# Cross-attention and feed-forward kernel: context rows transposed by DMA instead of by TensorE

## What is computed

```
x = x + mlstm_cell(layernorm(x), ctx, ctx)       # gated, causal, 4 heads of 64
x = x + layernorm(x) @ ternary(W).T              # 256 x 256
x = x + softmax(q @ k.T / 16) @ v                # q = layernorm(x) @ Wq; k, v = ctx @ Wkv
x = x + bitlinear(silu(gate) * up, w_down)       # 1024 inner features, 8-bit rows, ternary weights
```

## Time and profile before

| | us |
|---|---|
| median of 3 runs | 677.48 |
| the profiled execution | 679.77 |
| its span, first to last instruction | 677.9 |
| TensorE busy | 636.8 (94%) |
| VectorE busy | 568.9 (84%) |
| ScalarE busy | 524.9 (77%) |
| GpSimd busy | 394.2 (58%) |

### The profile page before, as it was taken

One profiled execution on the slowest core, in us unless ns is written; L12 is line 12 of the kernel. 1 busy time (PEld: TensorE's weight loads), 2 busy tenths in 40 slices (PEclk: granted clock), 3 DMA queues, 4 the chain that ended last, 5 costly groups with the idle time before them and its releaser, 6 DMA issues.

```text
span 677.9 us, 14933 instructions
## 1 busy us (share of the span) xinstructions
PE 636.8 (94%) x4689; PEld 475.0 (70%) x4710; DVE 568.9 (84%) x1481; ACT 524.9 (77%) x1302; POOL 394.2 (58%) x636
## 2 busy tenths in 40 slices
PE   5889999999999999999999999989799999999995
PEld 4668788787887878878778787777355555555563
DVE  4787978888898898887988889887899998899892
ACT  4666787887877869688687777766589988988984
POOL 3355464464644746547455474472467787777775
PEclk9999999999999999999999999999899999999997
DMA  8310202122022120221212201024336868766763
GB/s 297 108 57 7 94 1 94 57 70 95 16 95 72 54 95 20 92 83 44 94 40 87 94 17 64 19 60 156 71 71 163 171 156 170 136 164 160 167 133 110
DMA packets 105409, 63.64 MB, mean 94 GB/s; under 512 B 52845, under 2 KB 105070, under 8 KB 105334
## 3 DMA queue, kind: packets, MB, share of 16 engines
q1 hardware_dynamic: 98470, 59.29, 32.5%
q10 hardware_dynamic: 6864, 3.41, 1.7%
HBM read 29.39 MB, written 20.97 MB: 74 GB/s over the span
## 4 chain that ended last, share of the span: by engine, by line
PE 60%; DVE 14%; ACT 13%; DMA 5%; issue 4%; SPq 2%; POOL 1%; POOLq 0%; DVEq 0%; ACTq 0%
PE bank L704 10%; PE bank L621 9%; PE bank L672 8%; PE bank L651 8%; PE bank L723 5%; DMA us<-usq 4%; PE bank L693 4%; ACT ew L865 4%; PE bank L526 3%; PE bank L589 3%; ACT x2T L832 2%; PE bank L580 2%; DVE st L1239 2%; PE bank L665 2%; PE bank L571 2%
## 5 line engine op out<-in xcount | busy, mean ns | idle before, releaser
L704 PE MATMUL bank<-WGU,fqT 128*128 128x512 bf16 x491 | 122.0, 383 | 7.3 <-DVE vg L1544 3.7
L1110 POOL TENSOR_SCALAR_AFFINE_SELECT D<-D 128x512 f32<-128x512 f32 x64 | 38.4, 636 | 127.4 <-ACT D L856 127.4
L1544 DVE SCALAR_TENSOR_TENSOR vg<-bank,fback,D 128x1024 f32<-128x1024 f32 x64 | 82.0, 1281 | 11.8 <-ACT D L1016 5.7
L704 PEld LDWEIGHTS bank<-WGU,fqT 128*128 128x128 bf16 x512 | 46.9, 98 | 61.5 <-DVE vg L1544 24.0
L1016 ACT ACTIVATE D<-bank,fback 128x1024 f32<-128x1024 f32 x64 | 71.7, 1120 | 19.6 <-PE bank L704 19.6
L1551 DVE TENSOR_REDUCE hmax<-vg 128x1 f32<-128x1025 f32 x64 | 78.1, 1221 | 2.2
L1095 POOL TENSOR_TENSOR rs<-ve,minus_half 128x4 f32<-128x4 f32 x64 | 65.3, 1027 | 22.8 <-DVE ve L1245 20.4
L1196 POOL TENSOR_SCALAR wtmp<-vg,hscale 128x1024 f32<-128x1024 f32 x64 | 71.6, 1119 | 5.8
L1239 DVE BATCH_NORM_STATS2 st<-x 128x6 f32<-128x256 f32 x184 | 64.4, 411 | 2.7
L672 PE MATMUL bank<-W0T,x1T 128*128 128x256 f32 x256 | 60.1, 388 | 2.6 <-DVE C L1346 2.6
L651 PEld LDWEIGHTS bank<-vaug,C 128*128 128x128 f32 x512 | 60.7, 192 | 2.1 <-issue 1.3
(11 more groups left out here) (198 smaller groups left out, 1524.1 us busy)
## 6 DMA issues: line engine op xcount, KB each, us to landing
out_dram<-x SPq DMA_DIRECT2D x30, 512.0 KB, 3.3
xg<-in_x_dram SPq DMA_DIRECT2D x16, 512.0 KB, 3.9
cg<-in_ctx_dram SPq DMA_DIRECT2D x16, 512.0 KB, 4.5
xg<-out_dram SPq DMA_DIRECT2D x8, 512.0 KB, 4.7
cg<-out_dram SPq DMA_DIRECT2D x8, 512.0 KB, 5.5
rows_q<-fq ACTq DMA_DIRECT2D x13, 256.0 KB, 2.3
raw<-in_L_ffn_w_gate_dram SPq DMA_DIRECT2D x1, 1024.0 KB, 8.2
nrm<-in_L_ffn_w_up_dram SPq DMA_DIRECT2D x1, 1024.0 KB, 10.2
```

What stands on the lines that cost most here:

```text
L704: mm = pe.matmul(ps[k + half], fqT[:, i // 2 % 2, c, i % 2 * P:(i % 2 + 1) * P], WGU[:, c, which, half * 512:(half + 1) * 512], start=(c = ...
L1544: dve.scalar_tensor_tensor(out=fh[i % 2][:, 0:INNER], in0=up, scalar=fback[:, g % 2, s, 1:2], in1=fsil[:, i % 2, :], op0=ALU.mult, op1=ALU ...
```

## The change

- From turn n = 2 on, TensorE no longer transposes ctx (TC leaves the body of the loop; it stays in turns 0 and 1), and ScalarE no longer copies it.
- ScalarE, at the end of turn n, splits ctx of group n + 1 into its low and high 16-bit halves (split_ctx, two copies of 128x1024 into ctx_halves).
- SyncE issues two transposing DMAs (ctx_transposes) of 128x1024 16-bit elements, from ctx_halves into halves_turned (the memory of fhT). They stand between load and load_x of the same group.
- GpSimd joins the halves in qcT (join_ctx, two copies), behind power(0) and shifts(0) of turn n. TensorE's VG waits for it.
- T1 becomes the first stage of a turn, with its copies first on ScalarE. A turn has 46 bank uses instead of 48, so the banks rotate, and the banks after the loop are renumbered.

```diff
-STAGES = ("TB", "TC", "DX", "MB", "QK", "T1", "F0", ...
-NEW = {"TC", "TX", "VG", "GA", "TA"}
+STAGES = ("T1", "TB", "TC", "DX", "MB", "QK", "F0", ...
+NEW = {"TX", "VG", "GA", "TA"}
...
+        ctx_halves = sb("ctx_halves", [P, 2, GB * E], U16)
...
+        halves_turned = flat(fhT).bitcast(U16).rearrange("p (w k t) -> p w k t", w=2, t=P)
...
+            def ctx_transposes(g):
+                hold("sp", sp, ctx_split, 2 * g - 2)
+                for w in range(2):
+                    sp.dma_start_transpose(halves_turned[:, w, :, :],
+                                           ctx_halves[:, w, :]).then_inc(ctx_turned, 16)
...
                     load(z + 3, 1 - p)
+                    ctx_transposes(z + 3)
                     load_x(z + 3, 1 - p)
                     store(z)
...
                         for b in range(GB):
                             o = open_("VG", b)
-                            moved("TC", b // 2)
+                            if "TC" in bank.stages:
+                                moved("TC", b // 2)
+                            elif b == 0:
+                                pe.wait_ge(ctx_joined, 2 * n - 2)
...
+            def split_ctx(g):
+                pg = g % 2
+                act.wait_ge(c_in[pg], 8 * (g - pg) + 16)
+                if g > 2:
+                    act.wait_ge(ctx_turned, 32 * (g - 2))
+                for w in range(2):
+                    src = flat(cg).bitcast(U16).rearrange("p (q i w) -> p q i w", q=2, w=2)[:, pg, :, w]
+                    act.activation(ctx_halves[:, w, :], src, ACT.Copy).then_inc(ctx_split, 1)
...
+                if z is not None:
+                    turned_copies(bank, "T1", x1T)
                 if m is not None:
                     key_copy(bank, "TB", keyT[q][:, 1, :])
...
-                if n is not None:
+                if "TC" in bank.stages:
                     half_copies("TC", EC)
...
-                if z is not None:
-                    turned_copies(bank, "T1", x1T)
...
                 if y is not None:
                     scale_rows(y, (2, 3))
 
+                if n is not None and 1 <= n < NG - 1:
+                    split_ctx(n + 1)
...
+            def join_ctx(g):
+                pool.wait_ge(ctx_turned, 32 * (g - 1))
+                for w in range(2):
+                    dst = qcT[g % 2][:, EC:2 * EC, :, :].bitcast(U16).rearrange("p c b (t w) -> p b c t w", w=2)[:, :, :, :, w]
+                    pool.tensor_copy(dst, halves_turned[:, w, :, :].rearrange("p (b c) t -> p b c t", c=EC)).then_inc(ctx_joined, 1)
...
                     power(0, n)
                     shifts(0, n)
+                if z is not None and n is not None:
+                    join_ctx(n)
```

More of the change, by code:

```diff
@@ L35 @@
 BF16 = mybir.dt.bfloat16
-STAGES = ("TB", "TC", "DX", "MB", "QK", "T1", "F0", "UA", "TX", "UB", "VG", "T2", "SC", "TA", "GA", "WT", "O",
+U16 = mybir.dt.uint16
+STAGES = ("T1", "TB", "TC", "DX", "MB", "QK", "F0", "UA", "TX", "UB", "VG", "T2", "SC", "TA", "GA", "WT", "O",
           "WG", "WU", "WD")
-NEW = {"TC", "TX", "VG", "GA", "TA"}
+NEW = {"TX", "VG", "GA", "TA"}
 MID = {"TB", "DX", "MB", "QK", "UA", "UB"}
@@ L115, in last_places @@
     count = [sum(1 for i in range(start) if i % BANKS == k) for k in range(BANKS)]
-    one, two = (4, 5, 6, 7), (0, 1, 2, 3)
-    a = Places({"TB": (6,), "DX": (7, 0, 1, 2), "MB": (3,), "QK": (4, 5, 6, 7), "T1": two, "UA": (4, 5), "UB": (6, 7),
+    one, two = (0, 1, 2, 3), (4, 5, 6, 7)
+    a = Places({"TB": (2,), "DX": (3, 4, 5, 6), "MB": (7,), "QK": (0, 1, 2, 3), "T1": two, "UA": (0, 1), "UB": (2, 3),
                 "F0": two, "T2": one, "SC": one, "WT": one, "O": one}, count)
@@ L120, in last_places @@
     return a, b
-assert (len(FIRST) + len(SECOND) + sum(len(body(z)) for z in range(NG - 2))) % BANKS == 6
+assert (len(FIRST) + len(SECOND) + sum(len(body(z)) for z in range(NG - 2))) % BANKS == 2
 def build(nc, x, ctx_in, ig_w, ig_b, fg_w, fg_b, out_w, w0, wq, wkv, w_gate, w_up, w_down, out):
@@ L281, in build @@
         vaug_ready = sem("vaug_ready")
+        ctx_split = sem("ctx_split")
+        ctx_turned = sem("ctx_turned")
+        ctx_joined = sem("ctx_joined")
         gstep = sem("gstep")
@@ L356, in hold @@
             eng.sem_inc(held[name], 1)
-        bG, bU, bank_o = 4, 6, [ps[2], ps[3]]
+        bG, bU, bank_o = 0, 2, [ps[6], ps[7]]
         gate, up = (banks[:, k:k + 2, :].rearrange("p k n -> p (k n)") for k in (bG, bU))
-        bank_h = [ps[k].bitcast(F16) for k in (0, 1)]
+        bank_h = [ps[k].bitcast(F16) for k in (4, 5)]
         x2_last, x3_last = hh, qn
@@ L411, in _ @@
             load(2, 0)
+            ctx_transposes(2)
             load_x(2, 0)
@@ L419, in _ @@
             load(NG - 1, 1)
+            ctx_transposes(NG - 1)
             load_x(NG - 1, 1)
```

## The result

The changed kernel takes 775.23 us (median of 4 runs, 772.52 to 776.66) beside 677.76 us for the kernel before on the same chip: ratio 1.1425, 95% interval 1.1398 to 1.1452. It is 14% slower, +97.5 us. The profiled execution has a span of 773.2 us against 677.9. The forecast was 755, with a range of 715 to 792.

The account below looks back on a forecast made before the run. A turn was taken as a TensorE-bound front plus a back of about 12 us chained through three engines. Late x 5.0 and clock 0.3 us, by 14 turns, plus 3 us gave +77: 755 us, range 715 to 792.

Parts of the forecast that it names:

- Queue order, the step that decides: SyncE: load of x waits behind split and two transposing issues, issuing at 222.7 instead of 214.45, landing at 226.8.
- The links of the loop: ScalarE's end, split, SyncE, x, VectorE, GpSimd, qn, VG, ScalarE's end: a closed loop, 32.6 us long.
- the sum: All turns: 5.0 us late x plus 0.3 clock, by 14 turns 74 us, plus 3 for weight copies: +77.
- Two terms of that link: SyncE and DMA: each transposing issue 2.1 us (bounds 1.19, 2.38); x landing 4.1 us after its issue (3.9, 5.3).
- The clock: TensorE at half clock behind its gap before UA, most of it hidden: 0.3 us a turn, bounds 0 and 1.5.
- Rival 3: TensorE stays at half clock through UA, TX, UB and much of VG: 2 us a turn, 783 us; chance 0.08.
- The low end of the sum: Issues of 1.19, landing 3.9, no clock cost: 3.0 us a turn, 42 us, 720 us.
- the high end: Issues of 2.38, landing 5.3, split 2.5, clock 1.5, join 0.5: 9.3 us a turn, 130 us, 810 us.
- TC's gain: TensorE: eight transposes fewer per turn from n = 2, 0.87 us; 12.2 us in fourteen turns if nothing else is late.
- T1's move: T1's eight transposes go from behind QK to the turn's head, their ScalarE copies first; ScalarE's change put at nothing.
- rival 2: The halves are late, not x: VG waits for transposes or GpSimd's join; 32 us more, 787 to 790; chance 0.10.
- Rival 1: The load of x isn't late enough to matter, TC's transposes are simply won: 665 us; chance 0.04.

Follow-up runs that it names:

- 1: The changed kernel with SyncE issuing load_x ahead of the two transposing DMAs of the same group: 675.92 us, ratio 0.9977 to the kernel before.
- 6: The changed kernel with unused 128x512 matmuls added ahead of F0 in every turn: 789.71 us with ten, 736.55 us with four.
- 4: The changed kernel, load of x still late, with T1 and its copies back behind QK and the decays: 793.38 us, ratio 1.1712.
- 9: The kernel of 1 with GpSimd's power(0), shifts(0) ahead of power(1), and ScalarE's split ahead of weight copies and last two scale_rows: 668.32 us.
- 5: The kernel before with load_x behind the store in SyncE's queue, without split, transposes or join: 738.34 us, ratio 1.089.

## Why the prediction was right, and where it wasn't

**Queue order, the step that decides: right, and shown.** The exchange in 1 removes the whole loss, and nothing else differs between the two kernels. The links of the loop, the first two from the turn at 293, the others from the short turn before it: end of scale_rows to x landed 291.10 to 300.65, 9.55 us (10.4 in the sum); x to qn 3.85 (3.8); qn to VG 6.4 in the short turn (5.7); VG to ScalarE's end 12.0 there (12.7). They add up to 31.8, and turns with little or no time at the low clock take 31.0 to 31.7, where the sum had 32.6. TensorE's gap in front of UA is 3.6 us in the mean (46.7 by 13), not 4.5 to 5.

**Two terms of that link were mis-sized.** A transposing issue takes 1.32 us and not 2.1: the price is nearly one per instruction, the lower of the two bounds. It was the row of 1.19 us at half the size and not the doubling of it that held. The 1.9 us that the prediction estimated from the Trainium skill, page "DMA: Bandwidth & Descriptors", section "Why a DMA increments its semaphore by 16 and not by 1", was too high as well: the issues here took 1.32. Two issues make -1.6 us a turn. The other way, the load lands in a median of 4.7 us instead of the 4.1 taken, inside its bounds:

```profile
L418 SPq DMA_TRANSPOSE fhT<-ctx_halves x28: 1232/1320/1413, 48.0 to 505.1; - x28
```

```profile
L413 SPq DMA_DIRECT2D xg<-in_x_dram x14: 521/526/1497, 50.7 to 506.5; - x14
...
DMA to landing us min/median/max: 4.2/4.7/5.4
```

**The clock: the term that was furthest off.** The sum had 0.3 us a turn, bounds 0 and 1.5; the runs show 2.7 in the mean (38 by 14), above the dear bound. I had read three microseconds at half clock behind a gap of 2.37 from the one place in which the kernel before shows it, carried the length over, and called most of it hidden, because ScalarE comes to UA's products late. Here the low level lasts 3.4 us in one turn and 13.7 in another, after gaps of nearly the same length. What works at half speed in the long ones is exactly the chain from UA to VG, on which ScalarE waits: qn to VG takes 9.0 us there (6.4) and VG to ScalarE's end 14.2 (12.0). Rival 3 had the mechanism and nearly the price, 2 us a turn more than the sum where it is 2.4, with a chance of 0.08. Why one turn gets the clock back after 3.4 us and the next after 13.7 stays open.

The Trainium skill, page "TensorE: Matmul & The Clock Gate", section "HAM oscillation — how this bites in real kernels", says that the half rate comes back in every pass of a loop in which TensorE idles between bursts. The trace agrees: the granted clock is 0.77 to 0.95 in each of the 13 turns. What it would cost here had to be measured.

**Whole sum.** At full clock the change costs 736.55 - 676.91 = 59.6 us (6, which still has the late x), where the sum without its clock term had 73; the clock costs 38, where it had 4. The errors, -13 and +34, cancel in part, and the time came out 20 us above the forecast and inside a range that was made wide for the unknown prices. That is partly luck: 775.2 lies just above the narrower range, 720 to 775, to which I had given most of the chance, and without the first error it would have come near 789. (The low end of the sum, 720, also leaves out the 3 us of the turns with weight copies that the high end has.)

**TC's gain and T1's move.** TC's 0.87 us a turn is TensorE time, and with the queue mended 0.65 of it arrives (27.60 to 26.95). "At nothing" for T1's move was wrong: alone it costs 6.8 us, by the way from its copies over decays, GpSimd's powers and qn to the gate rows. I had followed ScalarE's own idle time and not who waits for the decays. In the change itself the move helps (4), since F0 then runs inside the wait for x.

**ScalarE and GpSimd.** The split takes 1.90 us (2.0 in the sum). In the turns without weight copies it is covered, as forecast: nobody waits for ScalarE at the head there. The join takes 2.6 us (2.3) and ends well ahead of VG in all turns looked at; rival 2 fell. Rival 1, the load not late enough to matter, fell by the 6.2 us mean wait at VectorE. In the three turns with weight copies the split isn't covered: TensorE stands up to 2 us at the T1 copies behind it, and moving the split won 5.6 us in all (9), where the sum had 3 for these turns.

## What to carry to other kernels

SyncE's queue issues in order, and a transfer that waits holds up what stands behind it: before putting one into it, look at what stands behind it, when that is wanted, and move the one with the early reader in front. A gap that a late load opens on TensorE costs more than its own length, as the granted clock falls at its end or shortly behind it and part of the chain there runs at half speed; price that from both ends, and if in doubt fill the gap as an experiment. A saved operation is won only as far as the next waits allow: banks, GpSimd's order and the place of a copy decided here whether 0.87 us of TensorE time came through.

## What the runs showed of the hardware that was not expected

- The issue of a transposing DMA took nearly the same time at two sizes: 1.19 us for 128x512 elements of 16 bits, 1.32 us for 128x1024.
- A plain load issued right behind two transposing DMAs takes 0.53 us to issue and lands in 4.7 us; in the kernel of 1, where it stands ahead of them, the issue takes 0.37 us, as in the earlier trace rows, and the landing 3.9. In the kernel of 5, where it stands behind a store and no transposing DMA is near, the medians are 0.45 and 5.0 us, so the longer landing isn't peculiar to transposes. Why the issue is longer wasn't tried.
- After gaps of 3.5 to 3.7 us on TensorE, the 1.2 GHz level lasted between 3.4 and 13.7 us, with the same matmuls in the same order behind the gap.
- Copies of 128x1024 16-bit elements: 1.10 us on ScalarE, reading every other one, and 1.34 us on GpSimd, writing every other one (2.6 us for both of a join). On ScalarE that is no more than other operations of this size take; on GpSimd it is a fifth more than the earlier trace rows, and how much of that is the stride wasn't measured.
